# Two-part F32R copies of B and C, and the first gate folded into the output projection's weights

## The reference, cut to what matters

```python
x_dbl = xb @ x_proj_w                 # 16 columns of dt, 16 of B, 16 of C
dt = softplus(dt @ dt_proj_w + dt_proj_b)
decay = exp(dt[..., None] * A)
inp = dt[..., None] * Bm[:, :, None, :] * xb[..., None]
h = dc * h + ic                       # over the 512 rows, for each of 16 states
y = einsum('bdn,bn->bd', h, c)        # weighted by C, summed over the states
out = (y + xb * D) * zb @ out_proj_w  # 256 -> 128
x = x + ga * out                      # ga: one row of 128 values per sequence
```

## Time and profile before

| | us |
|---|---|
| median of 3 runs | 3630.56 (3628.31 to 3631.08) |
| the profiled execution | 3629.41 |
| its span, first to last instruction | 3627.6 |
| PE busy | 2920.3 (81%) |
| DVE busy | 2813.8 (78%) |
| ACT busy | 1952.1 (54%) |
| POOL busy | 888.7 (24%) |

### The profile page before, as it was taken

The page is one execution under the profiler, slowest core; times in us unless marked ns, Lnnn a source line. Parts: engine busy times, 40 slices in busy tenths (PEclk is TensorE's granted clock), DMA queues, the critical chain, the costliest instruction groups (busy, mean ns, idle before and its releaser), DMA issues. The chain is left out here.

```text
span 3627.6 us, 53483 instructions
## 1 busy us (share of the span) xinstructions
PE 2920.3 (81%) x15912; PEld 2143.3 (59%) x15912; DVE 2813.8 (78%) x4814; ACT 1952.1 (54%) x4744; POOL 888.7 (24%) x590
## 2 busy tenths in 40 slices
PE   2387889888988888888889867888888888888876
PEld 1164566556655665566556546666666666667665
DVE  3999999999999999999997246666666666666664
ACT  3466768676867686767675423333333333333332
POOL 0443333333333333333332000011111111111111
PEclk6588999999999999999999989999999999999998
DMA  2000000000000000000000020000000000000000
GB/s 103 8 4 14 17 19 3 19 16 19 3 19 19 16 3 19 19 16 3 16 17 17 12 74 10 17 16 16 16 16 16 16 16 16 16 16 16 16 8 11
DMA packets 49771, 64.31 MB, mean 18 GB/s; under 512 B 3584, under 2 KB 36416, under 8 KB 49184
## 3 DMA queue, kind: packets, MB, share of 16 engines
q1 hardware_dynamic: 47392, 54.93, 4.7%
q10 hardware_dynamic: 2304, 8.46, 0.6%
HBM read 41.78 MB, written 21.60 MB: 17 GB/s over the span
## 5 line engine op out<-in xcount | busy, mean ns | idle before, releaser
L789 POOL TENSOR_TENSOR acc<-acc,zz 128x1024 f32<-128x1024 f32 x256 | 608.4, 2376 | 1006.1 <-DVE h L1104 958.7
L1104 DVE TENSOR_TENSOR_SCAN h<-dec,u 128x1024 f32<-128x1024 f32 x256 | 585.4, 2287 | 13.2 <-issue 4.9
L918 PEld LDWEIGHTS bank<-one_sb,hid 128*128 128x128 f32 x4096 | 481.4, 193 | 30.9 <-issue 17.3
L918 PE MATMUL bank<-one_sb,hid 128*128 128x128 f32 x4096 | 483.3, 276 | 14.6 <-ACT hid L654 14.6
L866 PE MATMUL bank<-S,pick_sb 96*128 96x512 bf16 x512 | 209.4, 414 | 254.0 <-DVE zz L1116 141.0
L158 POOL TENSOR_SCALAR n_ve<-n_mv 128x4 f32<-128x4 f32 x96 | 54.4, 567 | 1360.2 <-DVE n_mv L141 1360.2
L622 ACT ACTIVATE dec<-dt,aneg 128x512 f32<-128x512 f32 (+1 forms) x512 | 341.4, 723 | 63.7 <-DVE h L1104 48.0
L1116 DVE TENSOR_TENSOR zz<-h,bank 128x1024 f32<-128x1024 f32 x256 | 312.5, 1221 | 10.5 <-PE bank L866 0.3
L866 PEld LDWEIGHTS bank<-S,pick_sb 96*128 96x128 bf16 x512 | 50.0, 98 | 447.5 <-DVE zz L1116 204.8
L1097 DVE TENSOR_TENSOR u<-dtx,bank 128x1024 f32<-128x1024 f32 x256 | 309.9, 1211 | 0.4 <-PE bank L866 0.3
L654 ACT ACTIVATE hid<-banks,one_sb 128x512 f32<-128x512 f32 x304 | 208.4, 691 | 106.5 <-PE bank L918 64.5
(11 more groups left out here) (265 smaller groups left out, 6975.8 us busy)
## 6 DMA issues: line engine op xcount, KB each, us to landing
kv_dram<-Gs ACTq DMA_DIRECT2D x16, 516.5 KB, 3.1
kvl<-kv_dram SPq DMA_DIRECT2D x16, 516.5 KB, 3.6
xs<-in_x SPq DMA_DIRECT2D x16, 256.0 KB, 2.8
x<-in_x SPq DMA_DIRECT2D x16, 256.0 KB, 2.9
x_dram<-x SPq DMA_DIRECT2D x16, 256.0 KB, 2.1
h_dram<-hT SPq DMA_DIRECT2D x16, 256.0 KB, 2.0
h<-h_dram SPq DMA_DIRECT2D x16, 256.0 KB, 2.6
x2s<-x_dram SPq DMA_DIRECT2D x16, 256.0 KB, 2.7
```

What stands on the lines that cost most here:

```text
L789: pool.tensor_tensor(acc[:, :, :], acc[:, :, :], zz[:, k % 2, :, :], ALU.add)\
L918: last = pe.matmul(bank1(f"down{e}")[:, j * D:(j + 1) * D], hid[:, e % 2, f, j * P:(j + 1) * P], w2[:, e, f, :], start=(f == 0), stop=(f = ...
L1104: dve.tensor_tensor_scan(h[:, :, :].rearrange("p g t -> p (g t)"), dec[:, k % 2, :, :].rearrange("p g t -> p (g t)"), u[:, :, :].rearrange ...
```

## The change

B and C are kept in two parts instead of three: ACT rounds 64 rows to F32R (a 32-bit type that TensorE takes as one operand), DVE subtracts once (`split_low`, now in slot 13), and ACT copies to S. `split_mid`, `round_rest`, the tile Rb and the use of R for a rest go. The spreads multiply an F32R picking matrix of 64 rows (pick_r, made once by ACT) by the 64 rows of S. PSUM bank 7 comes free for dt_proj after the subtraction.

The gate: a new DVE operation, `gate_projection`, multiplies outw (256 values a partition) by ga into a new tile outg, in slot 1 of each step, ahead of the slot's scan. `out_proj` multiplies by outg and waits for it. `first_residual` adds the projection from PSUM to x1 in one operation. SP's wait ahead of the loads of the gates is now on outg.

```diff
-            S = sb("S", [P, T], BF16)
-            Sn = sb("Sn", [P, T], BF16)
+            S = sb("S", [2 * 2 * NS, T], F32R)
+            Sn = sb("Sn", [2 * 2 * NS, T], F32R)
...
-                            sp.wait_ge(*ao_ok(b, 0))
+                            sp.wait_ge(*outg_ok(b, 0))
                             sp.dma_start(ga[:, :], gate_rows[0, b].partition_broadcast(P)).then_inc(ga_in.sem, 16)
...
+                    act.activation(pick_r[:, :], pick_sb[0:64, :], ACT.Copy).then_inc(pick_ok, 1)
...
-                        act.activation(Sn[0:96, :], bank1("xdbl")[0:96, :], ACT.Copy).then_inc(s_hi.sem, 1)
-
-                    def round_rest(n):
-                        act.wait_ge(*s_rem(n, 1))
-                        act.activation(Rb[64:96, :], R[64:96, :], ACT.Copy).then_inc(s_remb.sem, 1)
+                        act.activation(Sn[:, :], bank1("xdbl")[0:64, :], ACT.Copy).then_inc(s_hi.sem, 1)
...
-                        act.activation(S[0:96, :], Sn[0:96, :], ACT.Copy).then_inc(s_ok.sem, 1)
+                        act.activation(S[:, :], Sn[:, :].bitcast(F32), ACT.Copy).then_inc(s_ok.sem, 1)
...
-                        pe.matmul(banks[which][:, :], pick_sb[:, at:at + 1].to_broadcast([96, P]), S[0:96, :],
+                        pe.matmul(banks[which][:, :], pick_r[:, at:at + 1].to_broadcast([64, P]), S[:, :],
...
                         free1(pe, "oproj", s)
+                        pe.wait_ge(*outg_ok(b, 1))
                         pe.wait_ge(*yz_ok(b, 1))
...
-                                                 outw[:, g, :], start=(g == 0), stop=(g == G - 1))
+                                                 outg[:, g, :], start=(g == 0), stop=(g == G - 1))
...
-                    def split_mid(n):
+                    def split_low(n):
+
                         dve.wait_ge(*s_hi(n, 1))
-                        dve.tensor_tensor(Sn[32:64, :], bank1("xdbl")[32:64, :], Sn[32:64, :], ALU.subtract)\
-                           .then_inc(s_mid.sem, 1)
-                        dve.wait_ge(*s_lo(n, 0))
-                        dve.tensor_tensor(R[64:96, :], bank1("xdbl")[64:96, :], Sn[64:96, :], ALU.subtract)\
-                           .then_inc(s_rem.sem, 1)
-
-                    def split_low(n):
-
-                        dve.wait_ge(*s_remb(n, 1))
-                        dve.tensor_tensor(Sn[64:96, :], R[64:96, :], Rb[64:96, :], ALU.subtract)\
-                           .then_inc(s_lo.sem, 1)
+                        dve.tensor_tensor(Sn[32:64, :], bank1("xdbl")[32:64, :], Sn[32:64, :].bitcast(F32),
+                                          ALU.subtract).then_inc(s_lo.sem, 1)
...
+                    def gate_projection(b):
+                        dve.wait_ge(*ga_in(b, 16))
+                        dve.wait_ge(*oproj(b, 0))
+                        dve.tensor_tensor(outg[:, :, :], outw, mid(ga[:, :], G), ALU.mult).then_inc(outg_ok.sem, 1)
+
                     def first_residual(b, a):
                         dve.wait_ge(*oproj(b, 1))
-                        dve.wait_ge(*ga_in(b, 16))
-                        dve.wait_ge(*x1_ok(b, 0))
-                        if a is not None:
-                            dve.wait_ge(*L1.turned(a, 1))
-                        dve.tensor_tensor(ao[:, :, :], bank1("oproj").rearrange("p (j d) -> p j d", j=J),
-                                          mid(ga[:, :], J), ALU.mult).then_inc(ao_ok.sem, 1)
-                        dve.wait_ge(*ao_ok(b, 1))
                         dve.wait_ge(*r_in(b, 16))
-                        dve.tensor_tensor(x1[:, :, :], x1[:, :, :], ao[:, :, :], ALU.add).then_inc(x1_ok.sem, 1)
+                        dve.tensor_tensor(x1[:, :, :], x1[:, :, :],
+                                          bank1("oproj").rearrange("p (j d) -> p j d", j=J), ALU.add)\
+                            .then_inc(x1_ok.sem, 1)
...
                                 if slot == 13:
-                                    split_mid(n)
-                                if slot == 14:
                                     split_low(n)
                             if n is not None and slot == NS:
                                 softplus(n)
+                            if b is not None and slot == 1:
+                                gate_projection(b)
                             if a is not None and k >= 0:
                                 scans(k, a)
```

More of the change, by code:

```diff
@@ L345, in adaln_depth2 @@
             pick_sb = sb("pick_sb", [3 * 2 * NS, 2 * NS], BF16)
+            pick_r = sb("pick_r", [2 * 2 * NS, 2 * NS], F32R)
             aneg = sb("aneg", [P, G, NS])
@@ L349, in adaln_depth2 @@
             ga = sb("ga", [P, D])
+            outg = sb("outg", [P, G, D])
             hT = sb("hT", [P, T])
@@ L356, in adaln_depth2 @@
             xc = sb("xc", [P, G, T])
-            S = sb("S", [P, T], BF16)
-            Sn = sb("Sn", [P, T], BF16)
+            S = sb("S", [2 * 2 * NS, T], F32R)
+            Sn = sb("Sn", [2 * 2 * NS, T], F32R)
             R = sb("R", [P, T])
             dtr = R
-            Rb = sb("Rb", [P, T], BF16)
             dt = sb("dt", [P, G, T])
@@ L370, in adaln_depth2 @@
             xh = sb("xh", [P, J, D])
-            ao = xh
             x1 = sb("x1", [P, J, D])
@@ L402, in adaln_depth2 @@
             thirty = sb("thirty", [P, P])
-            w_in, a_exp, a_neg, init, passed, w_high, w_low = (
-                sem(n) for n in ("w1_in", "a_exp", "a_neg", "init1", "passed1", "w1_high_ok", "w1_low_ok"))
+            w_in, a_exp, a_neg, init, passed, w_high, w_low, pick_ok = (
+                sem(n) for n in ("w1_in", "a_exp", "a_neg", "init1", "passed1", "w1_high_ok", "w1_low_ok", "pick_ok"))
             h2_high, h2_low = sig("h2_high", 1), sig("h2_low", 1)
@@ L410, in adaln_depth2 @@
             L3 = Norm(sb, sig, "n3", EPS_MOD)
-            (in_done, xraw, zsilu, conv, xc_ok, xdbl, dtr_ok, s_hi, s_mid, s_rem, s_remb, s_lo, s_ok, dtps, dtabs,
-             dtexp, dtln, dt_ok, dtx_ok, acc0, bb, cbc, dec_ok, u_ok, scan, z_ok, accum, yz_ok, oproj, ao_ok,
+            (in_done, xraw, zsilu, conv, xc_ok, xdbl, dtr_ok, s_hi, s_lo, s_ok, dtps, dtabs,
+             dtexp, dtln, dt_ok, dtx_ok, acc0, bb, cbc, dec_ok, u_ok, scan, z_ok, accum, yz_ok, oproj, outg_ok,
              x1_ok, chainA) = (sig(n, p) for n, p in (
                  ("in_done", 4), ("xraw", 2), ("zsilu", 2), ("conv", 2), ("xc_ok", 1), ("xdbl", 1), ("dtr_ok", 1),
-                 ("s_hi", 1), ("s_mid", 1), ("s_rem", 1), ("s_remb", 1), ("s_lo", 1), ("s_ok", 1), ("dtps", 2),
+                 ("s_hi", 1), ("s_lo", 1), ("s_ok", 1), ("dtps", 2),
                  ("dtabs", 2), ("dtexp", 1), ("dtln", 1), ("dt_ok", 1), ("dtx_ok", 1), ("acc0", 1), ("bb", NS),
                  ("cbc", NS), ("dec_ok", 2 * NS), ("u_ok", NS), ("scan", NS), ("z_ok", NS), ("accum", NS),
-                 ("yz_ok", 1), ("oproj", 1), ("ao_ok", 1), ("x1_ok", 1), ("chainA", G * (TAPS - 1))))
+                 ("yz_ok", 1), ("oproj", 1), ("outg_ok", 1), ("x1_ok", 1), ("chainA", G * (TAPS - 1))))
             (logits, lshift, lexp, gw, gturn, gT_ok, b2ps, b2_ok, up, hid_ok, down, taken, fsum, fgate, x2_ok,
@@ L454, in adaln_depth2 @@
             ring += [f"up{n}" for n in range(26, 32)] + ["ks0", "ks1", "g0", "g1"]
-            freed = {"oproj": (BEF, ao_ok, 1), "turn3": (YES, L3.out, 1), "back3": (YES, h3n_ok, 1),
+            freed = {"oproj": (BEF, x1_ok, 1), "turn3": (YES, L3.out, 1), "back3": (YES, h3n_ok, 1),
                      "turn2": (BEF, L2.out, 1), "gates": (BEF, gT_ok, 1), "b2": (BEF, b2_ok, 1)}
@@ L464, in adaln_depth2 @@
             freed.update({f"ks{s}": (YES, kss_ok, s + 1) for s in range(2)})
-            freed.update({"logits": (BEF, lshift, 1), "turn1": (NXT, L1.out, 1), "xdbl": (NXT, s_rem, 1)})
+            freed.update({"logits": (BEF, lshift, 1), "turn1": (NXT, L1.out, 1), "xdbl": (NXT, s_lo, 1)})
             freed.update({f"x{g}": (NXT, xraw, g + 1) for g in range(G)})
@@ L746, in step @@
                                     key_square(m, y)
-                            if n is not None and slot == 13:
-                                round_rest(n)
                             if a is not None and slot + 1 <= NS - 1:
@@ L824, in _ @@
                     pe.wait_ge(w_low, E0)
+                    pe.wait_ge(pick_ok, 1)
                     def turn1(n, s):
```

1 line of the change is left out of this document (removed).

## The result

| | before | after |
|---|---|---|
| median | 3630.82 (3628.31 to 3633.78, 4 runs) | 3719.46 (3718.38 to 3734.48, 4 runs) |
| ratio, 95% interval | | 1.0253 [1.0226, 1.0281] |
| profiled execution | 3629.41 | 3734.48 |

The change costs 89 us; 30 were predicted, and the time lies outside the range. The profiled execution of after is the longest of its four runs, 15 us above the median; sums over its span are to be read with that.

The account below looks back on a forecast made before the run. DVE, 95% busy, was taken as the bound in the first sweep, level with PE then ACT over 31 us. Terms of +2.3 us a step by 14, +32, and -2 outside gave +30 on 3629.4: 3660, range 3635 to 3676.

Parts of the forecast that it names:

- The spreads: PE's F32R picking matmuls: rate costs nothing, dearer weight loads mostly hidden, +0.1 us a step (0 to 0.5).
- The gate's wait: DVE ahead of scan 0 waits for ga, loaded late behind x2, then multiplies: +3.5 us a step, 14 times.
- What the stall gives back: POOL's root ends before the later scan, so DVE's n_xh is no longer hindered: -0.48 us a step (0 to -0.5).
- the residual: On DVE, L1131 goes, -0.72 us a step, and L1135's replacement takes 0.68 instead of 1.09, -0.41.
- the gate arrives in time: Rival: ga is there when DVE ends the step before, -0.8 us a step, 3617; 0.12 for all clearly below 3641.
- Waits for the projection: DVE's residual waits for PE's projection more often than 6 times, through a lower clock: +0.3 us a step (0 to 0.5).
- The split at 0 a step: Two DVE subtractions go, 1.37 us, but the wait at dt grows as much, to 1.5: 0 a step, bound -1.37.
- The split's time is kept: Rival: dt's wait grows by less than said, so 14 x 1.37 = 19 us come back: 3641; chance 0.18.
- The late start costs more than its length: Rival: lower PE clock and weight loads in the bounding chain, 3668, or later landings, 3679; chance above 3672: 0.12.
- The page with 2.15 us for a DMA: Rival: the skill's DMA time for ga takes 1.45 us off each step: 3640; chance 0.04.

Follow-up runs that it names:

- The early pair: Two kernels with ga's load asked for a step ahead: the change, early (3668.31 us) against the gate alone, early (3611.41 us).
- the late pair: Two kernels with ga's load as late as in the change: the changed kernel (3719.46 us) against the gate alone (3651.90 us).
- the gate alone, early: The gate alone with ga's load asked for a step ahead, as soon as its last reader is done: 3611.41 us, ratio 0.9956.
- the change, early: The changed kernel with ga's load asked for a step ahead, its F32R spreads still on 64 rows: 3668.31 us, ratio 1.0104.
- the gate alone: The kernel before with only gate_projection, outg and the short residual added, B and C still in three bf16 parts: 3651.90 us, ratio 1.0060.
- the three pairs with a late and an early load: ga's load late against a step ahead: gate edit only, 3651.90 and 3611.41 us; changed kernel, 3719.46 and 3668.31; F32R on 96 rows, 3661.71 and 3609.95.
- early, F32R on 96 rows: The changed kernel with spreads widened to 96 rows by zero picking rows and ga's load asked for a step ahead: 3609.95 us, ratio 0.9960.
- bf16, early: Early, F32R on 96 rows, but with two bf16 parts in place of F32R, so B and C are less exact: 3605.70 us, ratio 0.9936.
- F32R, late load: The changed kernel with its F32R spreads widened to 96 rows by zero picking rows, ga's load still late: 3661.71 us, ratio 1.0084.

## Why the prediction was wrong

**The step that failed** is "The spreads": "their rate costs nothing; the weight load takes 199 against 98 ns", "most are hidden", and with it **+0.1** a step (0 to 0.5). The early pair puts it at (3668.3 - 3611.4) / 14 = 4.1 us a step for the whole split, the late pair at 67.6 / 14 = 4.8; for the row count alone it is 58 / 14 = 4.1. The duration and the weight load of the earlier trace rows were read rightly, but they are not what a matmul costs its neighbours. The step's other ground, that "u and zz are read over 1 us after it", fell too: they waited 26.2 us for spreads. I compared a 96-row row with a 128-row row, found both near 410 ns, and took the coming 64-row one to be of the same kind. The diff names that number (`to_broadcast([64, P])`), and the trace of before had a row to warn of it: dt_proj, on 16 rows, whose two matmuls began at 1098.80 and the spread behind them at 1099.85: 1.05 us, where two of the experts' matmuls of 128 rows take 2 x 0.23. (Padded to 128 rows, they let the matmul behind the spread come 0.3 to 0.4 us sooner.)

The Trainium skill (TensorEngine Tiling (Array Packing), Key Properties) says that changing the tiling mode, not just the tile, drains TensorE, and its section When to Use Tiling names a contraction of up to 64 for row tiling. I didn't weigh it. The runs fit it: 96 rows among 128 cost no more than 128, 64 and 16 do. That the breaks are this drain isn't shown by a run; that they hang on the row count is. The page gives no price; here it is 0.40 us a spread in F32R and 0.28 in bf16.

**Where it decides** was half seen. The text said that over 31 us "DVE's list and the list of PE and then ACT are equally long to 0.17 us", and used this to give the split nothing; the same sentence made any longer PE instruction there count in full. Six spreads up to dt_proj make 2.4 us of each step, and the rest comes in the waits at Sn, u and zz. Between the gate alone, early, and the change, early, the waits at dt, Sn, u and zz grow by 25.7, 14.0, 14.4 and 11.6 us; less the 19.2 of the two subtractions that makes 46.5 of the 52.7 us between their profiled executions.

**The gate's wait**, +3.5: right. In the turn shown outg began 3.68 us after the load's issue. Idle time of 53.8 us in 15 (the 14 and the last, where no scan stands behind it), the longest 4.3, 0.42 for the operation, and 40, 51 and 52 us regained in the three pairs with a late and an early load, against 45 from the rows.

**What the stall gives back and the residual**: right in every duration (1.11, 0.69, L1131 gone). The reason for n_xh was too narrow: it isn't the stall, as the early gate shows, but that even a 0.43 us operation stands ahead of the scan. The rival "the gate arrives in time" counted the -0.48 too, though the text had no ground for it once the stall is gone. Its 3617 lies 7 above the nearest kernel (early, F32R on 96 rows, 3610). Three small terms can account for that, though no run takes them apart: it kept +0.3 for the projection (there 5.5 us in 7 waits, against 4.9 in 6) and +0.1 for the spreads, and left out that 0.09 of issue time goes (0.42 ahead of the scan before, 0.33 ahead of outg now).

**Waits for the projection**, +0.3: the sign I named, "more often than 6 times", holds barely in after (7 times, 4.9 us as before) and more clearly with the gate alone (13 times, 7.5), which is 0.2 a step.

**The gate's sum.** These terms make 14 x 2.2 = 31 us. The profiled execution of the gate alone spans 3657.8, 30 more than before's; its six runs have a median 22 above before's. But that execution is the second longest of its six. By the medians the terms together are 9 us too high, and no run tells which of them; the six runs spread by 20 us, the longer ones mostly at the lower granted clock (3643.9 us at 0.926, 3663.8 at 0.917).

**The split at 0 a step**: right for what it named. Where the subtractions go and 96 rows stay, the wait at dt grows by 17.6 (bf16, early), 18.0 (F32R, early) and 19.1 us (F32R, late load), against 14 x 1.37 = 19.2, and the time by -5.7, -1.5 and +9.8. That last figure rests on the gate alone, whose runs spread by 20 us. The rival "The split's time is kept" falls: at most 5.7 of its 19 us are. In after the later waits at dt are (42.8 - 11.8) / 14 = 2.2 us each, not the 1.5 predicted, because PE's chain grew too.

**The rivals.** "The late start costs more than its length" had a piece of the truth, weight loads in the bounding chain, capped at 0.4 us a step; the type's share, 22 us on 64 rows and 4 to 10 on 96, is 1.6 and 0.3 to 0.7 a step, and some of it may be that; no run separates it. The page with 2.15 us for a DMA falls: 16 landings of 3.3 to 4.8 us, median 3.6.

## What to carry to other kernels

A matmul's price is read start to start, from the one ahead of it to the one behind, among the neighbours that it will have, and a contraction height that the stream doesn't yet have (here 64 or 16 rows among 128) is priced by the nearest such place in the trace, start to start, not by the instruction's own duration. Padding the operand with rows of zeros back to 96 was worth 58 us. Ahead of fusing a factor into an operand that is read earlier, look at which queue position issues that factor's load: asked for a step ahead, the same fusion went from +22 to -18 us.

## What the runs showed of the hardware that I had not expected

- 64 rows are dearer than 96, by 0.40 us a spread among 128-row matmuls in F32R (1.09 us against 0.71 from the matmul ahead to the second behind, medians of some 80 places), 0.28 in bf16. It isn't the matmul itself: two 64-row spreads behind each other stand in after as

```profile
1078.78 0.73 PE L861 MATMUL bank<-S,pick_r 64*128 64x512 f32 x2
```

which is one 0.50 us row and the usual 0.23.
- Two F32R spreads on 96 rows behind each other take 1.02 to 1.03 us where two bf16 ones take 0.60 and two F32R ones on 64 rows 0.73. No run tells why, and it may be part of the 4 to 10 us that F32R costs on 96 rows.
